# Vision tower on one Trainium2 core, token stage: a ring of selected points of six chunks, and the steps of each pair of bins moved later in their engines' queues

## The reference

```python
# tokens, batch 64, 3 channels of 224 x 224
f = jnp.fft.fftshift(jnp.fft.fft2(images))            # cropped to 192 x 192
power_sorted = jnp.abs(f).reshape(B, C, CROP * CROP)[:, :, idx]   # idx: by distance from the centre
ps = power_sorted.reshape(B, C, NUM_BINS, BIN_SIZE)   # 16 bins of 2304 points
tokens = jnp.einsum('bnf,ef->bne', ps.transpose(0, 2, 1, 3).reshape(B, 16, -1), W) + b
tokens = jnp.concatenate([cls, tokens], axis=1) + _sinusoidal_pe(17, 192)[None]
...
h = _layernorm(h + _L0_attn_ref(h, ...))              # causal attention, 12 heads
h = _layernorm(h + _L0_ffn_ref(h, ...))               # attention, then top 2 of 8 experts, hidden 768
```

## Time and profile before

| | us |
|---|---|
| median of 3 runs | 984.91 (983.77 to 992.57) |
| profiled execution, its own time | 995.24 |
| its span, first to last instruction | 993.4 |
| PE busy | 779.3 (78%) |
| DVE busy | 542.4 (55%) |
| POOL busy | 522.3 (53%) |
| ACT busy | 503.0 (51%) |
| mean granted TensorE clock | 0.87 |

### The profile page before, as it was taken

One profiled execution on the slowest core, in us unless ns is written; L12 is line 12 of the kernel. 1 busy time (PEld: TensorE's weight loads), 2 busy tenths in 40 slices (PEclk: granted clock), 3 DMA queues, 4 the chain that ended last, 5 costly groups with the idle time before them and its releaser, 6 DMA issues. The chain is left out here.

```text
span 993.4 us, 16237 instructions
## 1 busy us (share of the span) xinstructions
PE 779.3 (78%) x5345; PEld 668.2 (67%) x5346; DVE 542.4 (55%) x992; ACT 503.0 (51%) x964; POOL 522.3 (53%) x407
## 2 busy tenths in 40 slices
PE   5999999999993065878888977986969763999940
PEld 5888888888882064778787975665546652999940
DVE  3899999999992232333342435785278631222224
ACT  1777777777775032443243444762478310555510
POOL 4577777777772376566765612793077615000034
PEclk9999999999997567989897896797989955999975
DMA  9644468547873664434444328000000062111112
GB/s 225 184 136 138 136 180 229 178 129 198 227 274 81 197 180 130 129 111 135 135 134 116 118 73 288 1 1 2 0 1 2 2 202 77 38 48 54 48 48 70
DMA packets 81497, 115.58 MB, mean 116 GB/s; under 512 B 11049, under 2 KB 61298, under 8 KB 81074
## 3 DMA queue, kind: packets, MB, share of 16 engines
q1 hardware_dynamic: 70066, 81.85, 28.0%
q0 software_dynamic: 11392, 33.24, 11.5%
HBM read 91.76 MB, written 23.30 MB: 116 GB/s over the span
## 5 line engine op out<-in xcount | busy, mean ns | idle before, releaser
L544 PE MATMUL psum<-power,tT 128*128 128x192 f32 x864 | 176.7, 366 | 82.2 <-DVE tT L647 62.0
L544 PEld LDWEIGHTS psum<-power,tT 128*128 128x128 f32 x864 | 164.4, 217 | 92.3 <-issue 68.1
L490 POOL DMA_INDIRECT rows<-power_table,rank_row x144 | 144.2, 1001 | 107.6 <-issue 41.2
L285 PE MATMUL ps<-dft,fold 112*112 112x97 f32 x1536 | 170.9, 266 | 19.8 <-POOL fold L252 11.4
L285 PEld LDWEIGHTS ps<-dft,fold 112*112 112x112 f32 x1536 | 165.3, 181 | 28.4 <-DVE folded L357 15.5
L259 POOL TENSOR_TENSOR ss<-uv 97x388 f32<-97x388 f32 x96 | 119.5, 1267 | 77.9 <-ACT uv L325 77.9
L647 DVE SCALAR_TENSOR_TENSOR tT<-rows,swaps,scaled 128x384 f32<-128x384 f32 x144 | 81.2, 615 | 133.4 <-ACT scaled L593 56.2
L252 POOL TENSOR_TENSOR fold<-img 112x896 f32<-112x896 f32 x48 | 102.0, 2126 | 14.1 <-DMA img<-in_x 7.9
L357 DVE TENSOR_TENSOR folded<-ps,far 112x388 f32<-112x388 f32 x192 | 98.5, 553 | 18.8 <-ACT far L313 18.8
L374 DVE TENSOR_TENSOR uv<-ps,odd 97x388 f32<-97x388 f32 x192 | 98.5, 554 | 14.3 <-ACT odd L318 12.7
L593 ACT ACTIVATE scaled<-rows,swaps 128x384 f32<-128x384 f32 x144 | 76.2, 608 | 59.3 <-DMA rows<-power_table,rank_row 46.4
(11 more groups left out here) (141 smaller groups left out, 1073.8 us busy)
## 6 DMA issues: line engine op xcount, KB each, us to landing
img<-in_x SPq DMA_DIRECT2D x48, 784.0 KB, 4.9
power_table<-power SPq DMA_DIRECT2D x16, 576.0 KB
power<-in_w_tok SPq DMA_DIRECT2D x3, 1728.0 KB, 10.2
power_table<-power SPq DMA_DIRECT2D x1, 4656.0 KB
power<-in_w SPq DMA_DIRECT2D x8, 579.0 KB, 8.7
power<-in_w SPq DMA_DIRECT2D x4, 1152.0 KB, 11.0
rows<-power_table,rank_row POOLq DMA_INDIRECT x144
expert_inputs<-zeros SPq DMA_DIRECT2D x1, 2304.0 KB, 18.6
```

The lines of the kernel that those rows point to most:

```text
L285: last = pe.matmul(ps1[0:HALF, j % 2, i, col:col + FREQ], fold[:, j // UPG % FOLD_RING, part, x0:x0 + HALF], dft[:, part * FREQ:(part + 1) ...
L490: pool.indirect_dma_start(out=rows[:, j % RING, half, :], out_offset=None, in_=table[0:RECORDS if j < PLAIN else ROWS, :], in_offset=bass. ...
L544: last = pe.matmul(ps[:, q % 2, 0:DIM], points[:, j % SWAPPED, c, s].rearrange("p h b -> p (h b)"), wt[:, c, s, chunk, :], start=(chunk == ...
```

## The change

The ring of selected points gets 6 chunks in place of 3, and lies in `power` (the half that held the third pass of the spectrum, behind `ends`) in place of `tT`. `finish` is written after chunk 3 of the next pair; `turn` before chunk 5, the copies after chunk 7, `project` before chunk 8, and `batch_qk` after chunk 1 of the pair after. The class token's batch (b = 0) goes from pair 1 to pair 0: its transposes before chunk 3, its copies after 4, its projection before 6, its `batch_qk` after 7. Behind the last chunk, ACT has one `batch_qk` more to do, that of pair 7. The number of instructions of each kind stays.

```diff
-    RING, SCALED, SWAPPED = 6, 3, 3
+    RING, SCALED, SWAPPED = 6, 3, 6
...
-    points = W["tT_all"].rearrange("p a n -> p (a n)").rearrange("p (r c s h b) -> p r c s h b", r=SWAPPED, c=CHANNELS, s=2, h=2)
+    points = points.rearrange("p (r c s h b) -> p r c s h b", r=SWAPPED, c=CHANNELS, s=2, h=2)
...
+    FINISH, TURN, COPIES, PROJECT = 3, 5, 7, 8
+
+    def at_step(q, chunk, cls_at, ring_at):
+
+        if q == 0:
+            return 0 if chunk == cls_at else None
+        return q if chunk == ring_at else None
+
     def turn_at(q, chunk):
-
+        return at_step(q, chunk, 3, TURN)
+
+    def copies_at(q, chunk):
+        return at_step(q, chunk, 4, COPIES)
+
+    def project_at(q, chunk):
+        return at_step(q, chunk, 6, PROJECT)
+
+    def qk_at(q, chunk):
         if q == 0:
-            return {}.get(chunk)
-        return ({1: 0, 5: 1} if q == 1 else {2: q}).get(chunk)
-
-    def project_at(q, chunk):
-        return turn_at(q, chunk - 2)
+            return 0 if chunk == 7 else None
+        return q - 1 if chunk == 1 and q >= 2 else None
...
-            b = turn_at(q, chunk - 1)
+            b = copies_at(q, chunk)
             if b is not None:
-                batch_copies(b if q == 1 else pair, b)
-            b = project_at(q, chunk - 1)
+                batch_copies(pair, b)
+            b = qk_at(q, chunk)
             if b is not None:
-                batch_qk(b if q == 1 else pair, b)
+                batch_qk(pair - (q - b), b)
 
         act.wait_ge(index_in, 32)
         by_pairs(act, step)
+        batch_qk(PAIRS - 1, PAIRS - 1)
         batch_copies(PAIRS, PAIRS)
         batch_qk(PAIRS, PAIRS)
...
-            if j // CHUNKS >= 1 and j % CHUNKS == 1:
+            if j // CHUNKS >= 1 and j % CHUNKS == FINISH:
                 finish(pair - 1, j // CHUNKS - 1)
...
+        points = power[:, 0, 2 * PATCHES * RECORD:][:, 0:12 * RECORD]
```

More of the change, by code:

```diff
@@ L390, in spectrum, with tokens_of_rings @@
     return program_sync, program_pool, program_tensor, program_scalar, program_vector, stored, root_done
-def tokens_of_rings(nc, ctx, sem, rank_row, swaps, index_in, a, table, raw, wt, wt_in, ends, W, xT, qk, spectrum_done):
+def tokens_of_rings(nc, ctx, sem, rank_row, swaps, index_in, a, table, raw, wt, wt_in, ends, points, W, xT, qk, spectrum_done):
     ps = W["psum"]
     sb = lambda name, shape, dt=F32: ctx.enter_context(nc.sbuf_tensor(name, shape, dt))
-    RING, SCALED, SWAPPED = 6, 3, 3
+    RING, SCALED, SWAPPED = 6, 3, 6
     rows = sb("rows", [P, RING, 2, RECORD])
     scaled = sb("scaled", [P, SCALED, 2, RECORD])
-    points = W["tT_all"].rearrange("p a n -> p (a n)").rearrange("p (r c s h b) -> p r c s h b", r=SWAPPED, c=CHANNELS, s=2, h=2)
+    points = points.rearrange("p (r c s h b) -> p r c s h b", r=SWAPPED, c=CHANNELS, s=2, h=2)
     in_normed = W["normed"].rearrange("p t e -> p (t e)")
@@ L534, in step @@
             if b is not None:
-                turn(b if q == 1 else pair, b)
+                turn(pair, b)
             b = project_at(q, chunk)
             if b is not None:
-                project(b if q == 1 else pair, b)
+                project(pair, b)
             if chunk == 0:
@@ L1496, in build @@
         with ExitStack() as second:
-            rings = tokens_of_rings(nc, second, sem, rank_row, swaps, index_in, a, table, raw, wt, wt_in, ends, layers[0], xT, qk,
+            rings = tokens_of_rings(nc, second, sem, rank_row, swaps, index_in, a, table, raw, wt, wt_in, ends, points, layers[0], xT, qk,
                                     spectrum_done)
```

## The result

| | before | after |
|---|---|---|
| median of 4 runs each, same chip | 988.74 (983.77 to 996.22) | 1002.43 (997.87 to 1008.15) |
| ratio, 95% interval | | 1.0131 (1.0074 to 1.0187) |
| profiled execution, its span | 995.24, 993.4 | 1002.49, 1000.5 |

What follows compares the result with a forecast made beforehand. The prediction took POOL and PE stalling each other in the token stage as the bound. POOL's view gave 25 - 4 = 21 us, PE's 12.6 to 19; it took 15, so 984.9 - 15 = 970 us, range 948 to 991.

Steps and rivals of the forecast that it cites:

- What bounds the kernel: Token stage, 255.6 us: POOL (190 us of work) and PE (160) stall each other; PE's results 5 to 7 us late under gathers.
- the moved steps: ACT's copies, `batch_qk`: one chunk more lead cuts thirteen POOL waits by at most 2.5 us each, 28.5 of 41.5 us.
- The ring of six: DVE may lead PE by 6 chunks; alone this would take the 14.5 us of POOL's waits behind DVE's own ring.
- Pair 0: Class token's `batch_qk` after chunk 7 of pair 0 meets a late projection: 3.5 us of gain lost, leaving 25 us.
- The end: Last gather to last keys, 18.6 us before: PE's larger arrears add 2 to 6 us, taken as 4.
- PE's view: PE's 21.0 us of waits for points: 12.6 can go; with clock savings 12.6 to 19 us, taken as 15.
- The saving from avoided gaps at half clock: PE's first chunk after a gap takes 3.87 us, not 1.97; three or four gaps avoided save some 6 us.
- The new buffer: Ring placed in `power` beside the weights: cost taken as 0, with 2 us as its bound either way.
- Slower: Rival, around 994 us, chance 0.17: longer bursts of gathers make PE lose 15 us of work, against 6 gained.
- No change: Rival, 979 to 990 us, chance 0.27: only quiet DMA queues heal PE's lateness, so more lead only puts stops off.
- Its variant: Variant of the no-change rival: PE's lateness belongs to profiling alone; at most a quarter of POOL's waits could be so.
- The floor: Rival, 944 to 955 us, chance 0.10: the lead suffices for nearly all waits, 37.5 us gained, 947 us.

Runs made afterwards that it cites:

- ring_only: Ring of six in its new place with the old order of steps, against the kernel before on a prompt chip: 948.00 us, ratio 1.0021.
- ring_only_2: Ring of six in its new place with the old order of steps, run again on another prompt chip: 947.53 us, ratio 1.0008 to the kernel before.
- before_again: The kernel before, unaltered, traced again on prompt chip 15: 946.3 us.
- before_spread: The kernel before with two 1.8 MB copies within HBM added in each pair, late chip 9: 998.04 us, single execution, against 983.06 for the kernel before.
- after_spread: The changed kernel with two 1.8 MB copies within HBM added in each pair, late chip 9: 1012.28 us, single execution; the kernel before took 983.06.
- after_again: The changed kernel, unaltered, on prompt chip 15: 951.08 us against 952.20 for the kernel before, ratio 1.0039.
- tied: PE made to wait at six places for gathers ahead of it, prompt chip: kernel before 1005.23 us, changed kernel 1009.85; ratios 1.0606, 1.0635 to unaltered before.
- fixed: 18 extra PE matmuls at each of six places, prompt chip: kernel before 957.89 us, changed kernel 959.31; ratios 1.0117 and 1.0132 to unaltered before.

## Why the prediction was wrong

I forecast 970 us, 15 us faster; it came out 13.7 us slower on the same chip, above the range.

**What bounds the kernel.** The reading held in the main for the chip of the trace: neither POOL nor PE full, each stalling the other, results late by 5 us and more, mostly until the gathers have landed. "5 to 7 us" was too narrow: the keys at 526.56 us came 8.3 us late, and four other results 1.2 to 3.1 us late while POOL went on. Two things in it were missed. The lateness isn't part of the kernel: the same instructions have none of it on six of the seven chips known by number (by trace on one, by the time of the kernel before on all), and there POOL's issue is the bound, with 203 us for the 190 computed. And the idle of PE inside the faltering (25 us under "issue" at single entries) was the price, more than its wait for points.

**The step that failed** is that of the moved steps: "the lead of the whole chain grows by one chunk at the places that matter most, which is 2.5 us of POOL's time for every wait. Cut by at most 2.5 us each, the thirteen waits lose 28.5 us". It holds PE's late results to be a fixed delay that more lead covers. But at six `batch_qk` the delay lasted until POOL had paused. More lead put the pause off, to 9.5 chunks in the mean in place of 4.4; PE crawled meanwhile (30 entries in 20 us), and the pause was longer when it came: seven of 6.4 us in the mean in place of thirteen of 3.2. The term itself was to shrink the waits behind `batch_qk` from 26.0 us, and they grew to 40.8. That the pause is what ends the delay is read from these six times and from the quiet in which PE recovers; no run on a late chip moved the pause by hand, so it is argued and not shown. The sum had noted this against itself ("less POOL idleness also means less time to catch up") and then let it only pull the value down to 15 us, where it should have changed its sign.

**The ring of six.** "Alone this would take the 14.5 us": this term came true in so far as none of POOL's pauses stands behind the ring any more. The waits view still puts 14.4 us of DVE on PE, where it had 21.4 in 17 waits, but in one wait only, which ends at 494.50, 2.4 us after ACT took the keys out, as those put down to ACT do. What went up is the other kind, by 14.8 us. Which of the two halves makes the bursts long stays open, since each ran alone on prompt chips only.

**Pair 0.** Right: `batch_qk` there came at 389.79 after 15.59 us of idleness. I had given 3.5 us for it; POOL's first two pauses of 5.2 us became one of 6.95, so the 3.5 us weren't gained and 1.75 more went.

**The end.** I expected 4 us more from the last gather to the last keys. It was 18.6 us before and is 18.3 now (588.2 to 606.5). Why PE's arrears didn't grow wasn't looked into.

**PE's view.** The want of points fell by 9.9 us (12.6 expected), so this term was right. What the view left out is what came in its place: 19.3 us more between entries of the projections and 5.9 us more between matmuls. The saving from avoided gaps at half clock, some 6 us, came for the points, whose 864 matmul entries took 169.7 us in place of 176.7, but the projections, with gaps between their entries, took 25.0 in place of 19.4; the granted clock is 0.84 in 362 to 607 us (0.86 before, in 362 to 594).

**The new buffer.** Zero, as taken, as far as prompt chips show it: `ring_only` and `ring_only_2` are at ratios of 1.0021 and 1.0008.

**The rivals.** *Slower* is what happened. Its mechanism and the point from which it decides were named much as the trace shows them; its 994 us was built on 13 bursts each longer by one chunk, 15 us lost and 6 gained. The bursts were fewer and twice as long: PE's idle time between entries grew by 25 us, and the end of its waits for points gave 10 back. What misled me in giving it 0.17 was that I asked in how many bursts 2.5 us would be lost, not what ends a burst. *No change* had half of this, "waits as long in sum but fewer, each longer", and is what a prompt chip gives, for another reason. Its variant, late results only while being traced, can't be the whole of it, since prompt chips were traced in the same way and had none. Whether tracing has a part in it on a late chip isn't settled: the four executions of after all have a span and a granted clock on record, as the profiled one of before has, and of the others of before nothing says that they ran untraced, so the 10.3 us between the profiled one and the median, by which I bounded it, don't separate the two. *The floor* of 947 us is close to what prompt chips give to either kernel (946 to 952), by the absence of lateness and not by a longer lead.

**What stays open.** What makes PE's results late on some chips, or in some sessions. On prompt chips neither more of PE's instructions nor heavy traffic before the gathers brings it about; traffic beside them, on a prompt chip, and an untraced run weren't tried. Of the change's parts and of a cap on POOL's lead nothing ran on a late chip, so what would win back the 13.7 us there is open.

## What to carry to other kernels

Before lengthening a ring, ask what ends the wait that it is to bridge: lead can cover a fixed delay (with one put in by hand the last gather came 6.2 us earlier, though the kernel was no faster), but not one that lasts until the producer pauses, and fewer, longer waits are the mark that such a delay seems to have left here. And a gap that ends when a whole group of transfers has landed should be read on a second chip before it is tuned against, since here it was worth some 40 us on one or two chips and nothing on six others, more than twice what the change moved.

## What the runs showed of the hardware that I hadn't expected

The same kernel takes 983 to 989 us in two sessions and 946 to 952 on six other chips, and the difference, where there are traces, lies in the stage with indirect gathers: last keys at 593.8 us against 552.2, with a mean granted clock of 0.86 there (362 to 594 us) against 0.99 (362 to 552 us of `before_again`). In the first trace of after, PE's entries under gathers come one in 2.1 us at worst. Other engines are released up to 8.3 us after the shown end of what they wait for in the first trace of before, and up to 11.7 us in that of after (9.9 and 11.2 in `before_spread` and `after_spread`); in the longest crawl this ended when the gathers had landed (DMA share 0.00 from 427 us). On these chips a gather takes POOL longer with the changed order: a mean of 1049 and 1056 ns against 1001 and 1010, with one of 3.40 us at 437.12 in the first trace of after. On prompt chips it is 1007 ns (`after_again`) against 1021 (`before_again`), and with lateness put in by hand 1026 against 1002 (tied) and 1012 against 1027 (fixed).
